# A router's running counts: eight to thirty-two products per row on TensorE, or three and a scan on VectorE

## The reference

```python
N = B * T                      # 4096 tokens
C = N // E                     # 512 places for each of 8 experts
logits = x @ Wr + br
probs = softmax(logits); gate = max(probs); idx = argmax(probs)
mask = one_hot(idx, E)
pos = cumsum(mask, axis=0) * mask        # the token's number among those of its expert
mask = mask * (pos < C)                  # tokens beyond 512 get nothing
# chosen tokens go through relu(x W1[e] + b1[e]) W2[e] + b2[e], times gate
```

## Time and profile before

| what | value |
|---|---|
| device time, median of 3 runs | 458.99 us (456.33 to 459.06) |
| span of the profiled execution | 493.5 us |
| TensorE busy | 372.6 us (75%), 1686 products |
| VectorE busy | 341.5 us (69%), 770 instructions |
| ScalarE busy | 240.5 us (49%) |
| GpSimd busy | 285.0 us (58%) |
| mean granted TensorE clock | 0.856 |

### The profile page before, as it was taken

How to read it: one execution, slowest core, us unless ns; L and a number is a source line. 1 busy time by engine, 2 the same in 40 slices (tenths; PEclk the granted TensorE clock), 3 DMA queues, 4 the chain that set the end, 5 groups by cost and what they waited for, 6 DMA issues and landing times.

```text
span 493.5 us, 5720 instructions
## 1 busy us (share of the span) xinstructions
PE 372.6 (75%) x1686; PEld 187.6 (38%) x1686; DVE 341.5 (69%) x770; ACT 240.5 (49%) x396; POOL 285.0 (58%) x196
## 2 busy tenths in 40 slices
PE   4889753676886977888439988885899878598692
PEld 3334310312412412424214355444566766244341
DVE  4898899999999999986220366763569855145341
ACT  2787835256556556626032338633687211336440
POOL 2142369699999999943724000178536665316764
PEclk9999955698788788799959999996789896579996
DMA  7114240872100100100302114211201121122201
GB/s 209 21 73 130 55 127 0 292 266 76 44 0 2 42 1 1 42 0 18 99 22 87 51 40 135 86 53 43 76 1 44 44 82 60 40 93 94 61 14 31
DMA packets 28555, 32.78 MB, mean 66 GB/s; under 512 B 5213, under 2 KB 20593, under 8 KB 28524
## 3 DMA queue, kind: packets, MB, share of 16 engines
q1 hardware_dynamic: 24268, 25.40, 16.6%
q0 software_dynamic: 3456, 6.31, 4.2%
q10 hardware_dynamic: 800, 0.71, 0.5%
HBM read 13.91 MB, written 19.38 MB: 67 GB/s over the span
## 4 chain that ended last, share of the span: by engine, by line
PE 37%; DVE 24%; issue 17%; ACT 9%; another core or an unknown queue 7%; POOL 3%; DVEq 2%; ACTq 1%; DMA 0%
DVE states L706 15%; PE ps L1539 5%; PE ps L1550 4%; PE ps L1758 3%; POOL states L851 2%; PE ps L1271 2%; PE ps L1003 2%; ACT scaled L1319 2%; PE ps L1859 2%; PE ps L1118 2%; PE ps L1542 2%; PE ps L1262 1%; PE ps L151 1%; PE ps L1844 1%
## 5 line engine op out<-in xcount | busy, mean ns | idle before, releaser
L851 POOL TENSOR_TENSOR states<-states,c_rows 128x1024 f32<-128x1024 f32 x60 | 143.5, 2427 | 18.9 <-DVE states L706 18.6
L706 DVE TENSOR_TENSOR_SCAN states<-ps,inp 128x1024 f32<-128x1024 f32 x64 | 140.5, 2259 | 0.2 <-issue 0.2
L700 ACT ACTIVATE ps<-ps,bias_p,scale_p 128x1024 f32<-128x1024 f32 x64 | 75.0, 1177 | 66.0 <-PE ps L694 65.9
L1092 POOL DMA_INDIRECT slots<-x,put x52 | 50.7, 975 | 49.1 <-DVE put L1086 35.2
L694 PE MATMUL ps<-stack,sel 96*128 96x512 bf16 x128 | 47.7, 466 | 40.2 <-DVE states L706 40.0
L1215 POOL DMA_INDIRECT x<-answers,put x24 | 23.6, 984 | 58.9 <-DMA answers<-reply 52.0
L1414 POOL DMA_INDIRECT out<-reply,home x32 | 31.8, 993 | 27.1 <-DVE reply L1391 19.1
L1391 DVE SCALAR_TENSOR_TENSOR reply<-ps,rows,kept 128x128 f32<-128x128 f32 x64 | 18.6, 344 | 30.7 <-PE ps L1271 19.4
L694 PEld LDWEIGHTS ps<-stack,sel 96*128 96x128 bf16 x128 | 9.1, 104 | 77.7 <-DVE states L706 71.3
L1508 ACT ACTIVATE d_hidden<-ps,b 128x512 f32<-128x512 f32 x24 | 16.4, 685 | 42.7 <-PE ps L1542 35.7
L728 PE MATMUL ps<-states,red 128*32 128x512 f32 x256 | 36.7, 679 | 0.2 <-POOL states L851 0.2
(11 more groups left out here) (199 smaller groups left out, 700.2 us busy)
## 6 DMA issues: line engine op xcount, KB each, us to landing
slots<-zero SPq DMA_DIRECT2D x8, 528.0 KB
rows<-slots SPq DMA_DIRECT2D x16, 264.0 KB
steps<-part SPq DMA_DIRECT2D x4, 768.0 KB, 3.3
stack<-steps SPq DMA_DIRECT2D x12, 256.0 KB, 4.2
answers<-x SPq DMA_DIRECT2D x4, 512.0 KB, 3.2
answers<-reply SPq DMA_DIRECT2D x8, 256.0 KB, 2.5
x<-in_x SPq DMA_DIRECT2D x3, 512.0 KB, 6.6
out<-x SPq DMA_DIRECT2D x3, 512.0 KB
```

Of the source, the lines that this page charges most:

```text
L700: act.activation(bank(ps, slot(b, u), 2), bank(ps, slot(b, u), 2), ACT.Exp, scale=m["scale_p"][:, group(u):group(u) + 1], bias=m["bias_p"] ...
L706: dve.tensor_tensor_scan(h[:, u * SEQ:(u + 1) * SEQ], bank(ps, slot(b, u), 2), inp[:, b * SEQ:(b + 1) * SEQ], 0.0, ALU.mult, ALU.add).then ...
L851: eng.tensor_tensor(h[:, u * SEQ:(u + 1) * SEQ], h[:, u * SEQ:(u + 1) * SEQ], c_rows[:, b * SEQ:(b + 1) * SEQ], ALU.mult).then_inc(done, 1)
L1092: pool.indirect_dma_start(out=m["slots"][n // BATCH], out_offset=bass.IndirectOffsetOnAxis(m["put"][:, b, i:i + 1], 0), in_=m["x"][:, b * ...
```

## The change

Sums over the tiles are made on VectorE and not by products. `onehot` is laid out expert by tile. Behind it a scan with 64 steps (a mask `run` that is 0 at each expert's first tile restarts it) writes `upto`: for each partition and expert, how many of its tokens up to tile i chose the expert. It raises a new semaphore `summed`. TensorE then needs three products per row: ones times `before` (the totals of all earlier rows for each partition, broadcast over the tiles; none in row 0), the triangle times `onehot`, and ones times `upto`. As `upto` includes the tile itself, the triangle's table is lowered by 1 everywhere. `place` gets a small operation, `carry`, which adds the row's totals to `before` (a copy in row 0, an addition in rows 1 and 2, nothing in row 3). `runs` fills the mask once with two memsets ahead of the first router. Products per layer: 80 before, 11 after.

```diff
-    t[:, C_TRI:C_TRI + P] = r[:, None] <= r[None, :]
+    t[:, C_TRI:C_TRI + P] = (r[:, None] <= r[None, :]) - 1.0
...
-            ("onehot", [P, BATCH, BT, EXPERTS], BF16),
+            ("onehot", [P, BATCH, EXPERTS, BT], BF16), ("upto", [P, EXPERTS, BT], BF16), ("before", [P, EXPERTS], BF16), ("run", [P, EXPERTS, BT], F32),
...
-        dve.tensor_tensor(m["onehot"][:, b, :, :], wide(m["first"][:, q, :]), rank, ALU.is_equal).then_inc(self.hot, 1)
+        dve.tensor_tensor(self.chosen(n), wide(m["first"][:, q, :]), rank, ALU.is_equal).then_inc(self.hot, 1)
+        dve.drain()
+        flat = lambda a: a.rearrange("p e i -> p (e i)")
+        dve.tensor_tensor_scan(flat(m["upto"][:, :, :]), flat(m["run"][:, :, :]), flat(m["onehot"][:, b, :, :]), 0.0, ALU.mult, ALU.add).then_inc(self.summed, 1)
         dve.drain()
...
+    def chosen(self, n):
+        return self.m["onehot"][:, n % BATCH, :, :].rearrange("p e i -> p i e")
+    def counted(self, n):
+        at = self.counts(n) * HALF
+        return self.ps[:, at:at + BT * EXPERTS]
+    def runs(self, dve):
+        dve.memset(m["run"][:, :, :], 1.0)
+        dve.drain()
+        dve.memset(m["run"][:, :, 0], 0.0)
+        dve.drain()
     def count(self, pe, n):
...
         need(pe, self.placed, n)
-        for row in range(b):
-            for i in range(BT):
-                pe.matmul(counts, m["ones"][:, :], m["onehot"][:, row, i:i + 1, :].broadcast_to([P, BT, EXPERTS]), start=row + i == 0, stop=False)
+        if b > 0:
+            pe.matmul(counts, m["ones"][:, :], m["before"][:, :].rearrange("p (e o) -> p e o", o=1).broadcast_to([P, EXPERTS, BT]), start=True, stop=False)
         need(pe, self.hot, n + 1)
-        pe.matmul(counts, m["tri"][:, :], m["onehot"][:, b, :, :].rearrange("p i e -> p (i e)"), start=b == 0, stop=False)
-        for i in range(BT - 1):
-            last = pe.matmul(self.ps[:, at + (i + 1) * EXPERTS:at + BT * EXPERTS], m["ones"][:, :],
-                             m["onehot"][:, b, i:i + 1, :].broadcast_to([P, BT - 1 - i, EXPERTS]), start=False, stop=i == BT - 2)
-        last.then_inc(self.count_psum, 1)
+        pe.matmul(counts, m["tri"][:, :], flat(m["onehot"][:, b, :, :]), start=b == 0, stop=False)
+        need(pe, self.summed, n + 1)
+        pe.matmul(counts, m["ones"][:, :], flat(m["upto"][:, :, :]), start=False, stop=True).then_inc(self.count_psum, 1)
+    def carry(self, dve, n):
+        if b == 0:
+            dve.tensor_copy(m["before"][:, :], m["upto"][:, :, BT - 1])
+        elif b < BATCH - 1:
+            dve.tensor_tensor(m["before"][:, :], m["before"][:, :], m["upto"][:, :, BT - 1], ALU.add)
...
         dve.drain()
+        self.carry(dve, n)
         dve.tensor_tensor(column(FACTOR), column(GATE), m["rstd"][:, self.use(n), tiles], ALU.mult)
...
         dense.minus_one(dve)
+        router.runs(dve)
         router.statistics(dve, 0)
```

More of the change, by code:

```diff
@@ L961, in __init__ @@
         self.logit_psum, self.count_psum = plan.sems("tensor", "r_logit_psum r_count_psum")
-        self.logit_read, self.below, self.hot, self.factored, self.placed = plan.sems("vector", "r_logit_read r_below r_hot r_factored r_placed")
+        self.logit_read, self.below, self.hot, self.summed, self.factored, self.placed = plan.sems("vector", "r_logit_read r_below r_hot r_summed r_factored r_placed")
         self.put_done = [plan.dma_sem(f"put{n}") for n in range(2 * BATCH)]
@@ L1042, in probabilities @@
         act.activation(self.m["prob"][:, n % 2, :, :], self.m["below"][:, n % 2, :, :], ACT.Exp).then_inc(self.exp, 1)
+    def chosen(self, n):
[4 more added lines that the diff above has]
+    def runs(self, dve):
+        dve.memset(self.m["run"][:, :, :], 1.0)
+        dve.drain()
+        dve.memset(self.m["run"][:, :, 0], 0.0)
+        dve.drain()
     def count(self, pe, n):
[L1047 to L1048 removed]
+        m, b, counts = self.m, n % BATCH, self.counted(n)
+        flat = lambda a: a.rearrange("p e i -> p (e i)")
         need(pe, self.placed, n)
[L1050 to L1052 removed]
+        if b > 0:
+            pe.matmul(counts, m["ones"][:, :], m["before"][:, :].rearrange("p (e o) -> p e o", o=1).broadcast_to([P, EXPERTS, BT]), start=True, stop=False)
         need(pe, self.hot, n + 1)
[L1054 to L1058 removed]
+        pe.matmul(counts, m["tri"][:, :], flat(m["onehot"][:, b, :, :]), start=b == 0, stop=False)
+        need(pe, self.summed, n + 1)
+        pe.matmul(counts, m["ones"][:, :], flat(m["upto"][:, :, :]), start=False, stop=True).then_inc(self.count_psum, 1)
+    def carry(self, dve, n):
+        m, b = self.m, n % BATCH
+        if b == 0:
+            dve.tensor_copy(m["before"][:, :], m["upto"][:, :, BT - 1])
+        elif b < BATCH - 1:
+            dve.tensor_tensor(m["before"][:, :], m["before"][:, :], m["upto"][:, :, BT - 1], ALU.add)
     def place(self, dve, n):
@@ L1070, in place @@
         need(dve, self.count_psum, n + 1)
-        dve.tensor_tensor(m["cum"][:, :, :], bank(self.ps, self.counts(n))[:, 0:BT * EXPERTS].rearrange("p (i e) -> p i e", e=EXPERTS),
-                          m["onehot"][:, b, :, :], ALU.mult)
+        dve.tensor_tensor(m["cum"][:, :, :], self.counted(n).rearrange("p (e i) -> p i e", i=BT), self.chosen(n), ALU.mult)
         dve.drain()
+        self.carry(dve, n)
         dve.tensor_tensor(column(FACTOR), column(GATE), m["rstd"][:, self.use(n), tiles], ALU.mult)
@@ L1457, in mark @@
         dve.drain()
-        dve.tensor_tensor(m["hot"][:, :, :], m["onehot"][:, self.n % BATCH, :, :], m["total"][:, :].rearrange("p (i o) -> p i o", o=1).broadcast_to([P, BT, EXPERTS]),
+        dve.tensor_tensor(m["hot"][:, :, :], self.router.chosen(self.n), m["total"][:, :].rearrange("p (i o) -> p i o", o=1).broadcast_to([P, BT, EXPERTS]),
                           ALU.mult).then_inc(self.hot, 1)
```

## The result

The change makes the kernel slower: 464.69 us (464.05 to 465.14, 4 runs) against 457.66 us of the kernel before in the same comparison (455.20 to 459.06, 4 runs), a ratio of 1.018 [1.015, 1.021]. Forecast were 461.6 us, a loss of 2.6 where 7 came.

A forecast was written before the change was run, and what follows sets the result against it. No single engine was taken to bound the whole; at counts 2 and 3 VectorE's chain is the later one. 1.9 + 0.37 + 0.09 + 0.37 - 0.15 = +2.6 us on 459.0 gave 461.6 us, range 455.5 to 465.

The forecast's parts named there:

- The base: Plain median 459.0 us, taken as free of the profiled trace's waits, which were ascribed to the profile's own records.
- rival (a): Waits around count(3) are real in plain runs too, giving 14.3 us back: 447 us; chance 0.12.
- The undisturbed schedule: Counts 2 and 3 without the waits: triangle of count(3) at 240.6 us, TensorE waiting 0.9 us for VectorE.
- Removal: 160 products become 22 in both layers; most lie in waits, so only -0.15 us, at count(4).
- The scan, carry and memsets: Added on VectorE: scan 0.30 us per router, carry 0.09 in rows 0 to 2, memsets and drains 0.30 before router 0.
- The layout: New order of `onehot`: costed at nothing, 0 to 0.07 us per operation that touches it.
- The first layer: VectorE's chain to count(3) and TensorE's wait for the scan: TensorE resumes 1.9 us later (1.1 to 2.8).
- rival (c): TensorE's clock falls behind the longer wait at count(3), costing 2 to 2.5 us: 464 us; chance 0.12.
- Its second place: The late dense part, behind the gap of router 7, also starts at a lower clock: 466 us.
- The middle: First layer's last sum to the first c_z: no term of its own, forecast 0 more.
- The second layer: Scan's 0.37 us at add(2) behind choose(5), carry of router 4 0.09, and 0.37 at router 7's `cum`.

The follow-up runs named there:

- e5: The kernel before once more, unchanged, in a series without the long waits: 456.07 us, ratio 1.001 [0.997, 1.004].
- e1: The kernel before once more, unchanged, in a series with the long waits: 492.83 us, ratio 0.999 [0.996, 1.003].
- e9: The kernel before with 400 unused bytes per partition declared where the change declares its three new tensors: 456.81 us, ratio 1.000 [0.997, 1.002].
- e4: The kernel after with all VectorE additions, but TensorE counting with the old products and not waiting for the scan: 495.84 us, ratio 1.007 [1.001, 1.013], long waits.
- e6: The kernel after once more, unchanged, in a series without the long waits: 465.22 us, ratio 1.021 [1.016, 1.026].
- e8: The kernel after with 8b - 1 idle early products in row b, without the long waits: 464.32 us, ratio 1.020 [1.014, 1.025].
- e10: The kernel after with 112 unused bytes more per partition behind its three new tensors: 465.77 us, ratio 1.020 [1.017, 1.023].
- e13: The kernel before with 15 idle drains on VectorE ahead of everything: 491.96 us, ratio 0.997 [0.993, 1.002], long waits.
- e14: The kernel after with 69 idle products on TensorE in an early pause: 489.73 us, ratio 0.996 [0.991, 1.001], long waits.
- e7: The kernel after with onehot written in memory order, without the long waits: 464.1 us, ratio 1.016 [1.011, 1.022].
- e17: The kernel after with the `run` array made by GpSimd at the start and nothing else: 496.87 us, ratio 1.011 [1.005, 1.018], long waits.
- e2: The kernel after with onehot written in memory order, in a series with the long waits: 489.86 us, ratio 0.993 [0.989, 0.997].
- e12: The kernel after with one-hot in memory order, `run` by GpSimd, 8b-1 idle products per row and 112 bytes more: 459.51 us, ratio 1.010 [1.006, 1.013].
- e11: The kernel before with only the new order of `onehot` in memory, no scan, carry or memsets: 456.68 us, ratio 1.002 [0.999, 1.005].

## Why the prediction was wrong

**The base, right for a wrong reason.** I took the waits of the earlier trace rows as absent from the timed runs and added to 459.0. They are absent there, so rival (a) fell. But they are not made by recording: e5 was recorded the same way and has a span of 455.2 us in an execution timed at 457.0, and in e1 the kernel before was itself timed at 490.6 to 493.7, waits and all. The Trainium skill's rule, NOTIFIC — the notification-queue block, section Constraints, capacities, measured rates (a record costs the engine no cycles), agrees with e5, whose recorded execution is no longer than the runs without the profiler (456.3 to 459.1). My mistake was the step from it to rival (a): that the waits belong to the program does not put them into every series. Hence also the span: 482 was forecast for after, and the series gave 463.1.

**The undisturbed schedule, about right.** The triangle of count(3) was put at 240.6 us with a wait of 0.9; e5 has 241.16 and 0.73. At count(2), where I had 0.90, e9 waits 0.91; e5, whose clock had just been down, does not wait.

**Removal worth next to nothing, right.** e4 with its 80 products and after with its 11 take the same from one-hot 0 to 1 (8.34 and 8.35 us) and from 1 to 2 (8.14 and 8.13). Even the 0.15 us that I took at count(4) are not there: its triangle had no wait in the earlier trace rows, but waits 1.13 us in e5 and 0.60 in e9.

**The scan, carry and memsets, right:** 0.29 for 0.30, 0.09 for 0.09, 0.28 for 0.30.

**The layout, a mis-sized term.** "I cost it at nothing, from 0 to 0.07 per operation": it was 0.22 us for each one-hot operation, 0.9 us in the first layer and some 0.6 in the second. From one-hot to `cum` I gave 1.1 us; it is 1.33. I had looked at sizes and types, and not at the order in which VectorE writes: 2-byte elements 16 bytes apart.

**The first layer.** With the memsets 1.9 us were forecast, with bounds of 1.1 to 2.8; at full clock it is 0.29 + 2.26 = 2.6, of which the layout is 0.9. The other 1.40 of e6's 3.66 are the clock. That is rival (c), with a chance of 0.12. The step that failed is "at the 0.9 us waits no fall is seen": the same paragraph puts the new wait ahead of count(3) at 1.9 us, and I left the clock out of the sum by what waits half as long had done. The wait is 1.89 in after, and the fall comes right behind it, for 1.6 us where I had 2 to 2.5. In e6 and e8 the wait is 1.06 and 1.18 and the fall does not come. What rival (c) did not have are the falls ahead of count(3), 2.00 us in e6 and 4.24 in e10. Its second place did not matter: the late dense part has 17.2 us at half clock in e5 and 17.0 in e6.

**The middle, a missing term.** I let the first layer's delay pass through unchanged. The change made this stretch 1.7 us longer without touching a line of it: 15 more VectorE instructions and 69 fewer TensorE products move two code transfers beside transfers that the path waits for. e13 and e4 show that the first moves, e14 beside e6, e7 and e10 that the second does and that the landing is short again; that these transfers are the cause of the delay is the reading that fits, with e17 as told above left to explain.

**The second layer.** 0.68 forecast, 2.42 measured. The one-hot operation's 0.22 at routers 4, 5 and 7 makes 0.66 of the gap. Router 4's scan may count too: the second c_z comes 1.15 us later than the first one's shift explains, and choose(4) and place(4) stand ahead of the work between them on VectorE, where I had let only 0.09 of it through. But before's own profiles e5 and e9 differ by 2.0 us in that stretch, so this is not shown. Nor are the 2.42 a fixed size: from the first c_z to the last sum before takes 130.2 (e5) and 129.5 us (e9), the change 132.6 (e6), 133.8 (after) and 130.9 (e10). These three have 10.3, 16.9 and 6.8 us at half clock between 324 and 388 us, where e5 has 5.3, so part of it may again be the clock; e9, with 10.3 there and the shortest time, speaks against it. The rest, about 1 us, I can't place.

Sum of the runs, e6 against e5: 0.3 memsets, 2.3 VectorE's chain in the first layer (0.9 of it the layout), 1.4 the clock there, 1.7 the middle, 2.4 the second layer: 8.1.

## What to carry to other kernels

Where TensorE's short products lie in a wait, taking them out gives nothing; and if the wait grows by the change, ask what the clock does behind a wait of the new length, not of the old one. A new layout is a price of the engine that writes it: look at the stride of the innermost step, not only at shapes. And a kernel whose path waits for small transfers can lose a microsecond or two far from the edit, because the number of instructions decides when program code is transferred; tell such a loss from a real one by putting idle instructions into the kernel before. Last, look at more than one profile of each kernel: the first layer of one and the same kernel had its falls of the clock at different places.

## What the runs showed of the hardware

- Writing 128x64 bf16 elements 16 bytes apart took VectorE 0.44 us, contiguously 0.225 (e2, e7, e12 against e6). Reading them so in the `cum` operation cost nothing (0.21 against 0.22 us).
- Program code comes as transfers of 16 KB (queue 8) and 8 KB (queue 14) among the data. One of 8 KB between the last `answers<-reply` and the first gather, 29.0 us behind the sum, goes with 0.43 us more until that gather starts, one at 29.3 with none and one at 30.0 with 0.64; one of 16 KB at the moment a gather lands goes with 0.4 to 1.3 us more of landing.
- Queue 8 has 14 transfers in before and 13 in after, which has 138 products and as many weight loads less.
- The granted clock fell behind waits of 1.69 to 1.89 us at count(3) (after, e7, e10) and not behind those of 0.73 to 1.18 (e5, e6, e8, e9, e11, e12). Of one kernel, after and e6, one execution had 3.4 us at half clock in the first layer and another 10.3.
- Waits without a named releaser add some 37 us (456 to 493), at places that depend on the moment: the kernels that pass the first c_z's stretch with their statistics at up to 43.3 us have one of 6.1 to 7.5 us there, those at 43.6 and later do not (e13 against e14, 43.7 and 43.3 in the table).
